# Selective-scan layer on one core: product units spread between the bursts, scalings and transfers moved to other engines

## The reference

```python
def step(carry, inp):
    z, s = carry
    u_t, dt_t, k_t, Bz_t, Bx_t, Cz_t, Cx_t = inp
    dtE = dt_t[:, :, None, None]
    S = 1.0 / (1.0 + dt_t[..., None] * k_t[..., None] + (dt_t * dt_t)[..., None] * A)
    z = S[..., None] * (z - dtE * A[None, :, :, None] * s + dtE * (Bz_t[..., None] * u_t[:, :, None, :]))
    s = s + dtE * z + dtE * (Bx_t[..., None] * u_t[:, :, None, :])
    y = jnp.einsum('bhn,bhnd->bhd', Cz_t, z) + jnp.einsum('bhn,bhnd->bhd', Cx_t, s)
    return ((z, s), y)
...
x = x + _layernorm(_L0_attn_ref(_layernorm(x, axis=-1), ...), axis=-1)
x = x + _layernorm(_L0_ffn_ref(_layernorm(x, axis=-1), ...), axis=-1)
```

## Time and profile before

| what | us |
|---|---|
| median of three runs (2732.02 to 2741.79) | 2736.1 |
| the profiled execution | 2735.51 |
| its span | 2733.8 |
| PE busy in the span | 2264.5 (83%) |
| DVE busy | 1873.4 (69%) |
| ACT busy | 1164.3 (43%) |
| POOL busy | 360.2 (13%) |
| mean granted TensorE clock, share of full speed | 0.843 |

### The profile page before, as it was taken

How to read it: one execution, slowest core, us unless ns; L and a number is a source line. 1 busy time by engine, 2 the same in 40 slices (tenths; PEclk the granted TensorE clock), 3 DMA queues, 4 the chain that set the end, 5 groups by cost and what they waited for, 6 DMA issues and landing times. The chain is left out here.

```text
span 2733.8 us, 56799 instructions
## 1 busy us (share of the span) xinstructions
PE 2264.5 (83%) x20514; PEld 1409.3 (52%) x20514; DVE 1873.4 (69%) x4268; ACT 1164.3 (43%) x2659; POOL 360.2 (13%) x540
## 2 busy tenths in 40 slices
PE   5766478898989898988989898989898997646886
PEld 2333225555555555554555555555555556635775
DVE  5776258776768677767777695867767776537765
ACT  3554225253544445352625354443525352203544
POOL 0000111111111111111111110111111110033210
PEclk9888788898989889988989898988888895557997
DMA  3554533434344343434443444434343433052410
GB/s 99 174 171 152 154 104 89 130 97 110 103 117 116 92 127 98 110 100 115 109 113 93 120 105 105 129 101 108 91 119 104 110 90 77 5 200 108 146 63 23
DMA packets 240312, 299.22 MB, mean 109 GB/s; under 512 B 127904, under 2 KB 144288, under 8 KB 231840
## 3 DMA queue, kind: packets, MB, share of 16 engines
q1 hardware_dynamic: 126688, 144.19, 17.7%
q10 hardware_dynamic: 95808, 113.56, 15.5%
q0 software_dynamic: 17536, 37.78, 5.1%
HBM read 240.85 MB, written 51.39 MB: 107 GB/s over the span
## 5 line engine op out<-in xcount | busy, mean ns | idle before, releaser
L642 PE MATMUL m_ps_a<-m_valT,m_w_bc 128*128 128x512 f32 x2048 | 1062.7, 672 | 68.9 <-DMA m_valT<-scratch_valT 35.5
L642 PEld LDWEIGHTS m_ps_a<-m_valT,m_w_bc 128*128 128x128 f32 x2048 | 426.8, 218 | 576.6 <-issue 566.7
L597 POOL DMA_DIRECT2D m_shear<-scratch_shear x512 | 277.1, 542 | 1800.8 <-DVE m_psi L1004 1609.2
L1000 DVE TENSOR_TENSOR m_prod<-m_psi,m_shear 128x128 f32<-128x128 f32 x1024 | 294.9, 288 | 36.5 <-ACT m_shear L771 11.7
L1004 DVE TENSOR_TENSOR m_psi<-m_psi,m_prod 128x128 f32<-128x128 f32 x1024 | 293.6, 287 | 17.2
L812 ACT ACTIVATE m_sq<-m_ps_a 128x512 f32<-128x512 f32 x256 | 153.2, 599 | 303.5 <-PE m_ps_a L642 237.0
L771 ACT ACTIVATE m_shear<-m_shear,m_A 128x64 f32<-128x64 f32 x512 | 135.8, 337 | 330.9 <-DMA m_shear<-scratch_shear 299.9
L698 PE MATMUL m_ps_g<-m_raw 32*64 32x64 f32 x8192 | 184.9, 249 | 73.0 <-DVE m_g L1108 59.2
L678 PEld LDWEIGHTS m_ps_k<-m_u,m_kT 64*128 64x128 f32 x1792 | 189.6, 196 | 68.0 <-ACT m_kT L838 42.4
L723 PE MATMUL m_ps_k<-m_raw,m_Xb 128*112 128x64 f32 x1024 | 177.0, 306 | 56.8 <-ACT m_Xb L856 56.8
L698 PEld LDWEIGHTS m_ps_g<-m_raw 32*64 32x64 f32 x8192 | 164.4, 159 | 100.2 <-issue 84.4
(11 more groups left out here) (146 smaller groups left out, 2897.7 us busy)
## 6 DMA issues: line engine op xcount, KB each, us to landing
m_scale<-scratch_norm SPq DMA_DIRECT2D x512, 128.0 KB, 3.2
m_w_bc<-in_w_bcT ACTq DMA_DIRECT2D x252, 256.0 KB, 3.0
m_shear<-scratch_shear POOLq DMA_DIRECT2D x512, 64.0 KB, 2.7
m_det<-scratch_ab ACTq DMA_DIRECT2D x64, 256.0 KB, 5.6
scratch_gateT<-gate SPq DMA_DIRECT2D x8, 1024.0 KB, 3.9
scratch_valT<-val SPq DMA_DIRECT2D x8, 1024.0 KB, 4.4
scratch_svgT<-svg SPq DMA_DIRECT2D x8, 1024.0 KB, 5.6
scratch_u<-p_u SPq DMA_DIRECT2D x8, 1024.0 KB, 7.6
```

Source lines behind the costliest of these rows:

```text
L597: pool.dma_start(shear[h * N:(h + 1) * N, w % 2].rearrange("p k g t -> p k (g t)"), spread(src)).then_inc(into.sem, into.step)
L642: mm = pe.matmul(ps_a[j % 2].ap(), w_bc[:, j, kt, :], valT[:, kt, :], start=(kt == 0), stop=(kt == KI - 1))
L1000: dve.tensor_tensor(prod.ap().rearrange("p k g r -> p (k g) r"), psi_kt[of_half][:, :, t, :], window.unsqueeze(2).to_broadcast([P, 2 * HAL ...
```

## The change

- PE: `LEAD` goes from 4 to 5, so that the unit order of a phase starts one later. Each group now has unit, transposes, unit, state terms. The scores of a group are interleaved with a unit in two halves, and one more unit follows each group's outputs.
- `state_terms`: in place of one matmul for four heads (128 stationary columns, 64 moving), of which the diagonal blocks are used, one matmul per head (32 stationary, 16 moving): 112 instructions for a group in place of 28. `copy_terms` then takes 4 copies in place of 8.
- ScalarE's scaling of the windows goes to VectorE: `scale_window`, one multiplication for each window, issued four steps ahead of the window's turn.
- y of a group is stored in one transfer (112 partitions with the padding rows) in place of four; `ffn` reads it in four transfers for each row in place of one.
- valT and e_end are loaded by SyncE, ab by GpSimd, in place of ScalarE. `det_logs` of a phase runs near the end of the phase before.
- VectorE's order is new, and so are ScalarE's and SyncE's to match.

The core of the diff (the declarations, the load functions that move unchanged and the semaphore counts are left out):

```diff
 
     def ns(elements):
...
+                def output_scales(b, group):
+
+                    sp.wait_ge(b_scaled.sem, b_scaled.at(b, group))
+                    load_scales(group % 2, 1)
+
...
+                    for half in range(2):
+                        more = not (last and half)
+                        first = half * HALF
+                        then = first + HALF
+                        if more:
+                            norm_rows(b, then)
+                            input_scales(b, then)
+                            load_e_end(b, half + 1)
+                            output_scales(b, then)
+                            norm_rows(b, then + 1)
+                            input_scales(b, then + 1)
+                            output_scales(b, then + 1)
+                            norm_rows(b, then + 2)
+                        if half == 0 and not last:
+                            sp.wait_ge(a_made.sem, a_made.at(b, UNITS - 1))
+                            load_valT(b + 1)
+                        if more:
+                            input_scales(b, then + 2)
+                            output_scales(b, then + 2)
+                            norm_rows(b, then + 3)
+                        if more:
+                            input_scales(b, then + 3)
+                            output_scales(b, then + 3)
...
                             hh = half + 1 + w // NW
+                            if w == NW and not (last and half):
+                                pool.wait_ge(det_used.sem, det_used.at(b, half))
+                                load_ab(b, half + 1)
                             if not (last and hh > 1):
                                 pool.wait_ge(shear_used.sem, shear_used.at(b, (half + 1) * NW + w - 2))
                                 load_shear(b, hh, w % NW)
...
+                    pe.sem_inc(narrow_next, 1)
...
-                                col = (tile * 2 + p_) * HP * DH
-                                mm = pe.matmul(ps_k[odd][:, col:col + HP * DH],
-                                               kT[rows, p_, tile * P:(tile + 1) * P],
-                                               u[rows, s, tile, :], start=True, stop=True, skip_group_check=True)
+                                for h in range(HP):
+                                    col = (tile * 2 + p_) * DH
+                                    mm = pe.matmul(ps_k[odd][h * N:(h + 1) * N, col:col + DH],
+                                                   kT[rows, p_, tile * P + h * N:tile * P + (h + 1) * N],
+                                                   u[rows, s, tile, h * DH:(h + 1) * DH], start=True, stop=True,
+                                                   skip_group_check=True)
                     mm.then_inc(dX_made.sem, dX_made.step)
...
@@ -700,7 +761,7 @@
                                                        start=(p_ == 0), stop=(p_ == 1), skip_group_check=True)
                             if tile == TT - 1:
                                 mm.then_inc(g_made.sem, g_made.step)
-                    product(b, unit, last)
+                        product(b, unit, last, pair * 2, pair * 2 + 2)
...
@@ -732,67 +793,31 @@
                     for half in range(2):
                         first = half * HALF
                         for i in range(HALF):
+                            products(b, unit, 1, last)
                             transposes(b, first + i)
-                            products(b, unit, 1, last)
+                            products(b, unit + 1, 1, last)
                             state_terms(b, first + i)
-                            unit += 1
-                            if i < HALF - 1:
-                                products(b, unit, 1, last)
-                                unit += 1
+                            unit += 2
                         scores_and_unit(b, first, unit, last)
-                        products(b, unit + 1, 3, last)
-                        unit += 4
+                        products(b, unit + 1, 1, last)
+                        unit += 2
                         for i in range(1, HALF):
                             scores_and_unit(b, first + i, unit, last)
                             outputs(b, first + i - 1)
-                            unit += 1
-                        products(b, unit, 2, last)
-                        unit += 2
+                            products(b, unit + 1, 1, last)
+                            unit += 2
                         outputs(b, first + HALF - 1)
...
                     for odd in range(2):
                         n = TT - odd
-                        for h in range(HP):
-                            heads = slice(h * N, (h + 1) * N)
-                            src = ps_k[odd][heads, 0:n * 2 * HP * DH].rearrange("p (c r d) -> p c r d", r=2, d=HP * DH)
-                            ins = act.activation(X[heads, odd:odd + 2 * n - 1:2, :, group % HALF, :],
-                                                 src[:, :, :, h * DH:(h + 1) * DH], ACT.Copy)
+                        for p_ in range(2):
+                            src = ps_k[odd][:, 0:n * 2 * DH].rearrange("p (c r d) -> p c r d", r=2, d=DH)[:, :, p_, :]
+                            ins = act.activation(X[:, odd:odd + 2 * n - 1:2, p_, group % HALF, :], src, ACT.Copy)
                         ins.then_inc(dX_ready.sem, dX_ready.step)
...
+                def store_y(b, group, more):
+
+                    act.wait_ge(y_ready.sem, y_ready.at(b, group * 2 + 1))
+                    act.dma_start(dram["yT"][b, group, 0:ROWS, :], y.ap()).then_inc(y_stored.sem, y_stored.step)
+                    if more:
+                        load_u(b, group + HALF)
...
+                        evacuated(1)
                         copy_kT(b, first)
                         evacuated(1)
-                        window(2)
                         copy_terms(b, first)
-                        det_logs(b, half)
                         evacuated(1)
                         copy_kT(b, first + 1)
                         evacuated(1)
-                        window(3)
                         copy_terms(b, first + 1)
+                        det_inverses(b, half)
                         evacuated(1)
-                        det_inverses(b, half)
                         copy_kT(b, first + 2)
                         evacuated(1)
                         copy_terms(b, first + 2)
                         evacuated(1)
-                        window(4)
                         copy_kT(b, first + 3)
                         evacuated(1)
                         copy_terms(b, first + 3)
-                        if more:
-                            load_e_end(b, half + 1)
-                        window(5)
                         evacuated(2)
                         block_states(b, first)
                         evacuated(1)
-                        window(6)
-                        evacuated(1)
-                        evacuated(1)
-                        window(7)
-                        finish(0)
+                        copy_y(b, first)
+                        block_states(b, first + 1)
+                        store_y(b, first, more)
+                        evacuated(2)
+                        copy_y(b, first + 1)
+                        block_states(b, first + 2)
+                        store_y(b, first + 1, more)
                         evacuated(1)
                         if more:
-                            act.wait_ge(det_used.sem, det_used.at(b, half))
-                            load_ab(b, half + 1)
-                        window(8)
-                        finish(1)
+                            det_logs(b, half + 1)
                         evacuated(1)
-                        window(9)
-                        finish(2)
-                        evacuated(2)
-                        finish(3)
+                        copy_y(b, first + 2)
+                        block_states(b, first + 3)
+                        store_y(b, first + 2, more)
+                        evacuated(1)
+                        copy_y(b, first + 3)
...
                     steps.n = 0
 
+                def scale_window(b, half, w):
+                    into = shear_in[w % 2]
+                    dve.wait_ge(into.sem, into.at(b, ((half * NW + w) // 2 + 1) * HP - 1))
+                    v = shear[:, w % 2, 0].rearrange("p (g c) t -> p g (c t)", g=HALF)
+                    of_groups = A[:, half % 2 * HALF:half % 2 * HALF + HALF].unsqueeze(2)
+                    dve.tensor_tensor(v, v, of_groups.to_broadcast([P, HALF, NC * W]),
...
                     t, w = i // 2, i // 2 // W
                     of_half, window = half % 2, shear[:, w % 2, :, :, t % W].rearrange("p k g -> p (k g)")
-                    if i % (2 * W):
-                        dve.wait_ge(steps.sem, steps.n)
-                    else:
+                    dve.wait_ge(steps.sem, steps.n)
```

(49 more changed lines are left out.)

141 lines of the change are left out of this document (59 added, 82 removed).

## The result

The changed kernel takes 2637.0 us (median of four runs, 2623.3 to 2645.5), the kernel before in the same session 2734.1 us (2727.4 to 2741.8). The ratio is 0.964, with a 95% interval of 0.959 to 0.969. I had forecast 2530 with a range of 2455 to 2705: the sign is right and the range holds the time, but the gain is 97 us and not 205. The profiled execution has a span of 2636.1 us.

A forecast was written before the change was run, and what follows sets the result against it. No engine is full: a phase of 126.0 us is set by waits passing between engines. 66.2 + 47 = 113.2 us a phase, 15 x -12.8 = -192, with -12, -3, +2 makes -205: about 2530 us, range 2455 to 2705.

The forecast's parts named there:

- M3 to M0: From the mask of group 3 to the next phase's mask of group 0: 66.2 us of DVE's work, no wait left.
- M0 to M3: From the mask of group 0 to that of group 3 in a phase: 47 us, set by PE's chain.
- Sum ... = 42.8 us: DVE's and SyncE's chain from mask 0 to the scaled inputs of n3 (next phase's group 3), 4 us shorter than PE's.
- the store and its return 2.3, four issues 1.7 and about 3 of landing: Trip of the scale factors from n3's norms to its inputs' scaling, over SyncE and DRAM: 7.0 us.
- Rival B: Waits go but are given back, clock may drop after PE waits for mask 0: phase 119.3, 2620 us; chance 0.24.
- the 0.85: Sign of the rival with waits given back: granted clock below 0.85 in `mix` with a long M0 to M3.
- State terms: One matmul per head: 2.4 to 2.5 us a group in place of 3.1, bounds 1.5 and 3.1; worth nothing in the sum.
- PE has 5 us to spare: Before scores 1, PE waits for mask 0 from 61 to 66 us: idle 5 us once a phase.
- Ahead of the first phase, -12 us: Norms of a group follow each other by 18 us in place of 26, two more scalings waited for: net -12.
- The last phase, -3 us: Last phase has no units and nothing to scale: between 0 and -12.8 us, taken -3.
- ffn and y, +2 us: Single store of y spares three issues; ffn's y in four transfers: between -1 and +4 us, taken +2.

The follow-up runs named there:

- e7: Kernel before with one part of the change alone, windows of the shear factors scaled by VectorE and not ScalarE; 2653.0 us, ratio 0.973.
- e5: Changed kernel, but behind the first group each W_bc tile load brings only a quarter of its columns (output not the layer's); 2569.1 us, ratio 0.943.
- e10: Changed kernel with VectorE's scalings and SyncE's gathers reordered so other work stands beside each trip of scale factors; 2530.9 us, ratio 0.927.
- e1: Changed kernel with mask 3 and the keys of the next group 0 moved ahead of the scaling of n3's inputs; 2639.2 us, ratio 0.966.
- e2: Changed kernel with the unit that follows the scores of group 0 multiplied three times over; 2618.6 us, ratio 0.957.
- e3: Changed kernel with state terms and their copies as before, 28 wide matmuls and 8 copies a group; 2596.3 us, ratio 0.949.
- e6: Changed kernel with the recurrence steps ahead of the first phase moved from before each group's norms to between norms and scalings; 2616.3 us, ratio 0.962.
- e4: Changed kernel with y stored in four transfers a group and loaded in one a row, as before; 2624.0 us, ratio 0.959.
- e11: e10 with wide state terms in all phases but the last, y as before, and the first-phase steps of e6; 2476.1 us, ratio 0.907.

## Why the prediction was right or wrong, point by point

- **M3 to M0, 66.2 us.** Right in the number: 67.1 on average. The waits for norms, logarithms and state terms went (37.3 us over the span for the norms). A part of it is luck: a new wait of 3.1 us a phase for n0's factors stands there, so that without waits the stretch would be some 64 us, 2 less than I summed. What I had wrong is whose merit that was. I gave it to `LEAD` and to the logarithms ahead of time, and entered ScalarE's relief at nothing; e7 shows that windows on VectorE alone bring M3 to M0 from 78.4 to 72.3 us and 77 us of the 97.
- **M0 to M3, 47 us: the step that failed.** It is 53.0 on average. The step is "Sum ... = 42.8 us. It is 4 us shorter than PE's, so PE's 47 holds": DVE's and SyncE's chain was the longer one. Walked at the mean times of the 14 phases, the 10.2 us that it has above 42.8 lie in three places. M0 to M1 took 14.3 us where I had 11.3: mask 1 waits 2.8 us for TensorE's outputs 0, behind the wait for mask 0 and the lower clock. From M1 to the scaled inputs of n2 it took 18.5 where I had 13.6: VectorE waits 4.3 us for n2's factors and 0.5 for ScalarE, and this trip of 12.6 us I had not priced as a wait at all, for I thought it covered by queries 3. The gather of n3 took the 8.6 us that I had. From n3's norms to M3 it took 11.6 where I had 9.3: the term "the store and its return 2.3, four issues 1.7 and about 3 of landing" was 7.0 forecast and 9.8 measured (medians of 15 trips). e5 gives the 7.0 back (6.75) with three quarters of the weight traffic gone. TensorE's own chain was near enough, as e10 shows (46.3 and 45.4).
- **The mask behind the wait.** I summed the chain up to the inputs of n3 and didn't ask what it holds up once it is late. Mask 3 is in the same stream. e1 shows that the mask's place is not the cause: the trip moves with it.
- **Rival B** comes nearest: 2620 us forecast, 2637 measured, waits given back and the clock down behind the wait ahead of scores 1. Its terms are not what was measured, though: it had M3 to M0 at 71.2 and M0 to M3 at 48.1, and they are 67.1 and 53.0; nor did the granted clock of the phases fall below the 0.85 that I had named as its sign (0.88). Filling the wait gains some 19 us (e2); the larger part is the uncovered trip (e10: 96 us in the 14 phases by the orders of VectorE and SyncE alone). I gave it 0.24.
- **State terms.** Forecast 2.4 to 2.5 us a group and worth nothing. They take 1.2 us (75.5 us / 64 groups), below my lower bound of 1.5, cost 41 us in the time (e3), and 28 us of gain in the last phase, which I had at 3, is theirs for the larger part (19.1). That PE has 5 us to spare there was right, and a quicker burst only made that idle time longer.

```profile
L738 PE MATMUL m_ps_k<-m_u,m_kT 64*32 64x16 f32 x7168 | 75.5, 184 | 17.5 <-ACT m_kT L861 17.3
```

The rule of the Trainium skill that I had set against this edit ("TensorEngine Tiling (Array Packing)", Instruction Overhead, some 60 cycles for a small matmul) gives, as an estimate, 2.8 us for a group. The row disagrees, 75.5 / 7168 = 10.5 ns an instruction; the edit lost all the same, by a way that the rule doesn't name.
- **Ahead of the first phase, -12 us.** Wrong sign: the norms follow each other by 22.9 to 25.5 us, not 18. I had counted the trip and left out the steps in front of it (some 9 us), which the order puts there. e6 takes them away and gains 19.4 us to the first M3.
- **The last phase, -3 us.** -27.9. I had said that it has no units and nothing to scale and took its gain for small. It is the phase with the largest waits of the kernel before, here from VectorE's timeline of before (start, length, [idle before]):

```profile
2321.41 4.57 DVE L1041 TENSOR_TENSOR_SCAN m_det<-m_carry,m_det 128x512 f32<-128x512 f32 x4 [12.94 <-ACT m_det L826]
...
2352.56 0.43 DVE L1143 TENSOR_TENSOR m_part<-m_X,m_coef 128x256 f32<-128x256 f32 x1 [13.44 <-ACT m_X L847]
```

The logarithms issued ahead remove the first, the quick state terms most of the second. The clock is 0.50 there, so each TensorE burst counts double.
- **ffn and y, +2 us.** +7.6, of which e4 takes back 8.5.
- **What can be laid side by side.** Windows -77 (e7), state terms +41 (e3), y +13 (e4). If they add, the rest of the change (orders, `LEAD`, logarithms, transfers on other engines) is worth 97 = 77 - 41 - 13 + 74, about -74 us, or -70 with the firm 8.5 us for y. That number is by difference and was not run by itself, and e11 beside e10 is a warning that such parts need not add.

## What to carry to other kernels

A price for a transfer holds for the traffic beside which it was read; before a sum rests on a round trip over DRAM, look at what else is on the DMA engines in the stretch in which it will stand, and put more work of the waiting engine beside it than the quiet price asks for. When two chains of a stretch come out within a few us of each other, the range belongs to the step that decides between them, and everything that stands behind it in the same stream is late with it. Shortening the bursts of an engine that already waited gained nothing here and cost 3.8 us a phase: look first at who ends its next wait, and take such an edit only where its result is waited for.

## What the runs showed of the hardware that I had not expected

- Four matmul instructions of 64 x 32 stationary elements and 16 columns take about as long together (4 x 10.5 = 42 ns) as two of the scores' instructions (185.9 us / 8192 = 22.7 ns each). At the lower clock of the last phase it is 6.5 us / 448 = 14.5 ns each. No run tells whether neighbouring tiles overlap.
- Weight loads that nobody waits for lengthen others' transfers: 64 KB in place of 256 KB for each brings the trip of n3 from 9.8 to 6.75 us and the kernel from 2637 to 2569 us. The mean DMA share of M0 to M3 falls only from 0.54 to 0.49 with it, so that share alone does not tell the length of a trip.
- More work can make the kernel faster, and the same work slower: three times a unit ahead of a wait of TensorE gained 18.5 us where TensorE idled 17.0 us a phase (granted clock 0.92 in place of 0.88 over the 14 phases), and cost 89 us where it idled 5.8.
